# Next turn's input stage moved behind layer 1's gated unit, and two PSUM banks per VectorE instruction

## The reference, cut to what matters

```
xn = layernorm(x)
x  = x + FAVOR(xn) + LOCAL(xn)
xn = layernorm(x)
x  = x + ATTENTION(xn) + MOE(xn)
```

## Time and profile before

| what | us |
|---|---|
| median of 3 runs | 2262.85 |
| lowest and highest of them | 2262.48 to 2275.0 |
| the profiled execution, its time | 2274.8 |
| the profiled execution, its span | 2273.0 |

### The profile page before, as it was taken

How to read it: one execution, slowest core, us unless ns; L and a number is a source line. 1 busy time by engine, 2 the same in 40 slices (tenths; PEclk the granted TensorE clock), 3 DMA queues, 4 the chain that set the end, 5 groups by cost and what they waited for, 6 DMA issues and landing times.

```text
span 2273.0 us, 43389 instructions
## 1 busy us (share of the span) xinstructions
PE 1854.6 (82%) x18044; PEld 1077.6 (47%) x18044; DVE 1381.7 (61%) x2973; ACT 766.9 (34%) x1401; POOL 293.7 (13%) x238
## 2 busy tenths in 40 slices
PE   1788898788887798877988779888797887988887
PEld 1445444454454553545535444455444554444544
DVE  1666557665566664766656655666556665576654
ACT  0332253223522236233252233422343323533234
POOL 0110101101111021011110111101101101011010
PEclk9998899998999999998999989998899988999889
DMA  4000200002000020000100020000200002000020
GB/s 171 1 1 2 33 2 6 1 2 33 7 2 1 2 33 7 2 1 14 22 6 2 2 29 7 6 1 3 33 2 6 1 2 33 3 6 1 2 28 7
DMA packets 27478, 29.79 MB, mean 13 GB/s; under 512 B 3524, under 2 KB 25844, under 8 KB 26740
## 3 DMA queue, kind: packets, MB, share of 16 engines
q1 hardware_dynamic: 27284, 27.01, 6.3%
HBM read 12.06 MB, written 2.36 MB: 6 GB/s over the span
## 4 chain that ended last, share of the span: by engine, by line
PE 51%; DVE 28%; ACT 6%; SPq 5%; DMA 5%; issue 5%; POOL 0%; ACTq 0%; DVEq 0%
PE bank L913 5%; SPq L414 4%; PE bank L697 4%; PE bank L903 3%; PE bank L729 3%; DMA phi<-parts 3%; PE bank L888 3%; DVE lc L1295 2%; DVE lrec L1365 2%; DVE lc L1347 2%; DVE ftm L1276 2%; PE bank L926 2%; PE bank L998 2%; PE bank L589 2%; DVE fp L1286 2%
## 5 line engine op out<-in xcount | busy, mean ns | idle before, releaser
L1522 DVE TENSOR_REDUCE amx<-bank 128x2 f32<-128x512 f32 x256 | 163.1, 686 | 76.1 <-PE bank L926 75.9
L1143 ACT ACTIVATE silu<-bank 128x512 f32<-128x512 f32 x144 | 84.2, 597 | 275.4 <-PE bank L888 263.3
L1511 DVE TENSOR_TENSOR mh<-bank,silu 128x512 f32<-128x512 f32 x144 | 98.8, 691 | 116.8 <-PE bank L903 108.5
L913 PEld LDWEIGHTS bank<-w_mw,mh 128*128 128x128 f32 x1152 | 151.0, 210 | 24.0 <-issue 24.0
L913 PE MATMUL bank<-w_mw,mh 128*128 128x128 f32 x1152 | 158.1, 297 | 0.0
L455 POOL TENSOR_TENSOR lc<-lc,ls 128x512 f32<-128x512 f32 x32 | 40.8, 1274 | 897.8 <-DVE lc L1295 895.8
L888 PE MATMUL bank<-xn2T,w_mw 128*128 128x512 f32 x288 | 145.6, 629 | 0.0
L1543 DVE RECIPROCAL ftm<-bank 128x512 f32<-128x512 f32 x16 | 53.7, 3358 | 145.2 <-PE bank L1005 145.2
L637 PE MATMUL bank<-hT,w_wqkv 128*128 128x512 f32 x256 | 119.0, 602 | 17.2 <-ACT hT L1034 11.0
L1295 DVE SCALAR_TENSOR_TENSOR lc<-bank,w_cols,w_rotary 128x512 f32<-128x512 f32 x128 | 93.4, 746 | 59.1 <-PE bank L637 59.1
L1353 DVE TENSOR_REDUCE lmx<-bank 128x4 f32<-128x512 f32 x128 | 79.6, 685 | 80.0 <-PE bank L697 80.0
(11 more groups left out here) (265 smaller groups left out, 3709.5 us busy)
## 6 DMA issues: line engine op xcount, KB each, us to landing
phi<-parts SPq DMA_DIRECT2D x96, 64.0 KB
lc<-parts SPq DMA_DIRECT2D x96, 64.0 KB
w_mw<-in_mw SPq DMA_DIRECT2D x3, 1152.0 KB
x_in<-in_x SPq DMA_DIRECT2D x8, 256.0 KB, 9.5
out<-res SPq DMA_DIRECT2D x8, 256.0 KB, 2.3
w_wqkv<-in_wqkv SPq DMA_DIRECT2D x1, 1536.0 KB
w_w<-in_w SPq DMA_DIRECT2D x1, 682.0 KB
w_rotary<-in_rotary SPq DMA_DIRECT2D x1, 512.0 KB
```

Source lines behind the costliest of these rows:

```text
L913: last = mm(bank_of("final")[:, t], mh[:, (2 * q + i) % 4, t], W["mw2"][:, ORDER[q], i, :], start=(q == 0 and j == 0 and i == 0), stop=Fal ...
L1511: V.tensor_tensor(mh[:, n % 4, :], bank_of("moe_u", n)[:], silu[:, n % 2, :], ALU.mult).then_inc(sem["moe_h"], 1)
L1522: V.tensor_reduce(amx[:, 2 * b:2 * b + 2, h], bank_of("att_max", n)[:].rearrange("p (t k) -> p t k", t=2), AX.X, ALU.max).then_inc(sem["at ...
```

## The change

It does two things.

**The input stage of the next turn** is cut into pieces that stand earlier. SP loads the next `x_in` at the start of a turn. VectorE takes its moments in layer 0's gated unit (`input_moments`, ahead of the wait for `glu_var_ps`); the reciprocal root is made by the same eight instructions as layer 0's (eight columns in place of four), and put aside (`input_root`). `input_scale` stands in layer 1 behind FAVOR's residual. TensorE's transposes and `favor_queries` stand behind layer 1's gated unit, ahead of the wait for the second norm; so do ScalarE's copies, while its squares (`query_squares`) come ahead of the fourth expert. `favor_values` stays where it was. To allow it, the second norm goes to `ftm`, `fqk` and its squares to `lv`, and `xw` takes `cen` in place of `xnT`.

**Two banks per instruction.** The eight banks are one tensor; `pair_of_banks` makes rings start at an even bank, so that two jobs which follow each other are neighbours. Rotation is two TENSOR_TENSOR of 128x1024 per pair in place of four of 128x512, with tables `rot` of scale times rotary that are made once ahead of turn 0 (16 instructions of 128x256). Masks are 128x768, scaling is 128x1024. The maxima of group 0 are two instructions; group 1 keeps four. The bank table changes with it.

```diff
@@ the table of jobs
+        def pair_of_banks():
+            turns_of["short"] += turns_of["short"] % 2
         def favor_jobs(*slot):
             if slot in FAVOR_AT:
+                pair_of_banks()
...
-                    job("favor_score", n, "favor_p", n + 1)
+                    job("favor_score", n, "favor_p", n // 2 + 1)
...
-                job("loc_rb", 4 * l + p, "loc_qk", 8 * l + 2 * p + 2)
+                job("loc_rb", 4 * l + p, "loc_qk", 4 * l + p + 1)
...
@@ TensorE
-                    pe.wait_ge(sem["favor_p"], now("favor_p", 4 * quad + 4))
+                    pe.wait_ge(sem["favor_p"], now("favor_p", 2 * quad + 2))
...
-                        pe.wait_ge(sem["loc_qk"], now("loc_qk", 8 * l + 4 * g + 4))
+                        pe.wait_ge(sem["loc_qk"], now("loc_qk", 4 * l + 2 * g + 2))
...
+                if it + 1 < TURNS:
+                    turn_input(it + 1)
+                    favor_queries(it + 1)
                 pe.wait_ge(*freed("xn2T"))
...
-                if it + 1 < TURNS:
-                    turn_input(it + 1)
                 att_project(it, 0)
-                if it + 1 < TURNS:
-                    favor_queries(it + 1)
                 att_den(1)
@@ ScalarE
-                        act.wait_ge(sem["loc_c"], now("loc_c", n + 1))
+                        act.wait_ge(sem["loc_c"], now("loc_c", n // 2 + 1))
...
+                if it + 1 < TURNS:
+                    turn_input(it + 1)
                 act.wait_ge(sem["xn2T_ps"], now("xn2T_ps", 1))
...
+                    if q == 3 and it + 1 < TURNS:
+                        query_squares(it + 1)
                     widen(q)
@@ VectorE
+            for l in range(DEPTH):
+                for qk in range(2):
+                    for i, (trig, half) in enumerate(((0, 0), (0, 1), (1, 0), (1, 1))):
+                        ins = V.tensor_scalar(rot[:, l, qk, i, :], W["rotary"][:, 2 * qk + trig, :],
+                                              W["cols"][:, 2 + 4 * l + 2 * qk + half:3 + 4 * l + 2 * qk + half],
+                                              None, ALU.mult)
+                    made(ins)
...
+                        for n in (4 * quad, 4 * quad + 2):
+                            dve.wait_ge(sem["favor_score_ps"], now("favor_score_ps", n + 2))
+                            V.tensor_tensor(fpt2[n % 8 // 2], two_banks("favor_score", n)[:, :, 0:384],
+                                            W["causal"][:].unsqueeze(1).broadcast_to([P, 2, 384]),
                                             ALU.mult).then_inc(sem["favor_p"], 1)
...
+                        dve.wait_ge(sem["loc_raw_ps"], now("loc_raw_ps", 2 * m + 2))
...
+                        V.tensor_tensor(halves(lc[:, c:c + 2, :]), raw, tabs(0), ALU.mult)
                         if m >= 2:
                             dve.wait_ge(sem["loc_rot"], now("loc_rot", 2 * m - 2))
...
+                        V.tensor_tensor(halves(lsb[m % 2][:]), raw, tabs(2), ALU.mult).then_inc(sem["loc_c"], 1)
...
+                        c = 4 * qk + 2 * g
+                        dve.wait_ge(sem["loc_rot"], now("loc_rot", 2 * m + 2))
+                        V.tensor_tensor(lc[:, c:c + 2, :], lc[:, c:c + 2, :],
+                                        bank_of("loc_rb", m).unsqueeze(1).broadcast_to([P, 2, T]),
+                                        ALU.mult).then_inc(sem["loc_qk"], 1)
...
+                            if g == 0:
+                                dve.wait_ge(sem["loc_max_ps"], now("loc_max_ps", 8 * l + h + 2))
+                                V.tensor_reduce(lmx[:, :, i:i + 2, 0].rearrange("p j i -> p i j"),
+                                                two_banks("loc_max", 8 * l + h).rearrange("p i (j k) -> p i j k", j=TT),
+                                                AX.X, ALU.max).then_inc(sem["loc_mx"], 2)
...
+                            if it + 1 < TURNS:
+                                input_scale(it + 1)
...
+                    elif it + 1 < TURNS:
+                        input_moments(it + 1)
                     dve.wait_ge(sem["glu_var_ps"], now("glu_var_ps", l + 1))
...
-                if it + 1 < TURNS:
-                    turn_input(it + 1)
                 for b in range(G):
                     share = ftm[:].rearrange("p t d -> p (t d)")
```

More of the change, by code:

```diff
@@ L147, in build @@
         for n, ap in w.items():
[L148 removed]
+            if n not in ("ones2", "rotary", "block8", "projT"):
                 W[n] = sb("w_" + n, list(ap.shape), ap.dtype)
@@ L386, in freed @@
                 i, before, ahead = AT[name, k]
-                by, count, turn = before if before else last_in[i]
+                by, count, turn, held = before if before else last_in[i]
+                if turn and before and it + 1 == TURNS and not ahead:
+                    by, count, turn, held = held
                 turn += it - ahead - (0 if before else 1)
```

136 lines of the change are left out of this document (77 added, 59 removed).

## The result

The changed kernel took 2325.63 us (median of 5, 2310.71 to 2330.14) where the kernel before took 2267.75 in the same session: ratio 1.0239, 95% interval 1.0209 to 1.027. On the 2262.85 of the forecast that is 2317. A second series gave 1.0227 (1.0193 to 1.0261). It is slower, as forecast; the forecast's 2302 was 15 us short on that scale. The profiled execution shown here was the fastest of its series (2310.71, span 2308.9, against 2274.8 and 2273.0), while the profiled execution of before was the slower end of its own, so the rows show 36 us of the 49 to 58 that the medians lost.

A forecast was written before the change was run, and what follows sets the result against it. The bound was one long hand-over between TensorE and VectorE. Terms of 46.4 us over 8 turns, -8.4 over 7 and +1 gave 39 over 2262.85, so 2302 us; range 2252 to 2326, the forecast's own 2285 to 2320.

The forecast's parts named there:

- Turn's end: Without transposes and query products ahead of the normaliser, it starts sooner: gain 2.2 us in 7 turns.
- Price of a double instruction: A 128x1024 VectorE product in a row takes 1.14 us, bounds 1.0 and 1.3; a 128x512 one takes 0.608.
- Rotation: Waiting for the second raw half and second square delays TensorE's sums: +1.2 us per turn in layer 0, +1.6 in layer 1.
- First maxima: Masks wait for scaling to free their banks, making scores or maxima later: +1.8 us per turn in layer 0, +1.2 in layer 1.
- Gated unit, layer 0: Moments of 1.55 us stand where VectorE was just in time; +0.8 in 7 turns, bounds +0.2 and +1.5.
- Scale: In layer 1 the input scale, ahead of a reciprocal the projection waits for, has no cover: +1.1 us in 7 turns.
- Clock behind the gated unit: Work added in TensorE's wait behind layer 1's gated unit partly keeps the clock up: gain 0.9 us in 7 turns, bounds 0 and 3.1.
- rival 1: The clock stays up behind the gated unit, giving 3.1 us per turn and not 0.9: 2287 us; chance 0.14.
- At nothing: No cost from ScalarE's squares ahead of expert 3, SP's earlier `x_in` load, its absence behind the stack's transfers, or VectorE's norm.
- Rival 4: The clock also falls ahead of layer 0's first scores, +1.9 us in 8 turns: 2317 us; chance 0.18.
- Rival 2: Faster: only VectorE's busy time counts, as double products reach ScalarE and TensorE in existing holes: 2211 us; chance 0.13.
- rival 3: Both signs cancel: the maxima's bank waits cost half, the squares 0.25 us; 2265 us, chance 0.15.

The follow-up runs named there:

- experiment 10: Kernel before with double rotation alone, plus one overwritten 128x512 product per turn in layer 1 ahead of the first sums; ratio 1.0139 to the kernel before.
- experiment 2: The change without its input stage: double rotation, masks, scaling and group 0's maxima with the new banks; 2347.85 us, ratio 1.0329 to the kernel before.
- experiment 3: Kernel before with double instructions in rotation alone, banks as before; 2310.17 us, ratio 1.0157.
- experiment 8: Changed kernel whole, with other banks for the scaling rows and one quad of FAVOR scores; 2328.26 us, ratio 1.0251 to the kernel before.
- experiment 11: Kernel before with other banks for layer 1's four scaling rows, an edit of the bank table alone; 2257.61 us, ratio 0.9941.
- experiment 1: Kernel before with the new input stage alone, single-bank instructions and banks as before; 2281.23 us against 2274.06, ratio 1.0032.
- experiment 7: Experiment 1 with the moments between layer 0's two output additions and the scale between layer 1's; 2265.55 us, ratio 0.9984 to the kernel before.
- experiment 5: Experiment 1 with two more overwritten 128x512 products per turn, in TensorE's waits in and behind layer 1's gated unit; 2270.78 us, ratio 0.9997 to the kernel before.
- experiment 12: Kernel before with the input stage's moments and scale in VectorE's waits and layer 1's scaling rows in other banks, no double instructions; 2246.49 us, ratio 0.989.
- experiment 4: Kernel before with double masks, scaling and group 0 maxima alone, rotation as before, banks dealt in pairs; 2310.35 us, ratio 1.0154.

## Why the prediction was right, and where not

The sign, and the time within the range, came out. Against its own steps:

*Turn's end, -2.2:* -2.17 in the turns concerned, in every kernel with the stage moved. Right.

*Price of a double instruction, 1.14 in a row:* four in a row took 4.60 (1.15 each), two took 2.35, a single one 1.217. Right; from PSUM it costs the same as from SBUF.

*Rotation, +1.2 and +1.6:* +1.09 and +1.57 in turns without a fall of the clock. Right, and experiment 10 shows the second by itself. What the step left out is that the clock can fall at the longer wait in layer 1 (experiments 2 and 3: 1.6 more in all turns). In the changed kernel it fell there only in the last turn (21.03 from the end of layer 0's gated unit to layer 1's root, where the other turns have 19.52), which lacks the input stage's moments. So the two parts of the change do interact, and through the clock.

*First maxima, +1.8 and +1.2:* +1.97 in the lowest turn, +2.04 in the mean, and +1.21. Right in size, in layer 1 with some luck: there the scores start 1.08 later behind the scaling and the last maximum comes 0.47 later behind the first, while the clock makes the scores shorter (4.1 to 4.6 in before, 3.1 to 3.4 in after) and part of what follows longer. Experiments 8 and 11 show the wait where the forecast had it.

*Gated unit, layer 0, +0.8:* mis-sized. It was 1.3 in the mean. The forecast gave the root's wait a cushion of 1.1 (L802 at 1513.28 "wanted" it then) and counted 0.4 there. The moments put `ra` 1.36 later in all seven turns. TensorE came to L823 1.92 behind `ra` in each of them; in before it came to L802 2.76 behind it in the turn shown, but 1.88 to 3.17 over the eight turns. So the cushion was 0.84 in the turn that the forecast read, and nothing in the turn of before in which the clock was at 1.00 throughout. Two turns of experiment 1 with the clock at 1.00 throughout, the third with the moments and the last without, take 38.12 and 36.29 from FAVOR's reciprocal to the unit's end: at the upper level the moments cost 1.8.

*Scale, +1.1:* +1.02 in the turns concerned; 0.00 once it was hidden (experiment 7). Right.

*Clock behind the gated unit, -0.9 of a possible -3.1:* this failed as a size. In the first profile all seven turns kept the upper level: -3.1, rival 1's mechanism, and one of the three signs (L877's passes at 1.9 in most turns) by which the prediction said it would be wrong. It is not a property of the added work, though: the same work kept it in some turns of experiment 1 only. Half of L877's loss, taken between the bounds, had no mechanism behind it and was wrong for this kernel; over the seven turns of experiment 1 the stretch gave 1.5 in the mean.

*At nothing:* ahead of turn 0 the +1 was not there: the table products lie wholly in the wait, and the first `w_w` product starts at 48.18 (48.14 in the earlier trace rows):

```profile
48.18 1.06 DVE L1230 TENSOR_SCALAR w_w<-w_w,w_cols 128x682 f32<-128x682 f32 x2
```

But the attention's maxima came 0.8 to 1.2 later per turn in each of the six kernels with the input stage moved (experiments 1, 5, 7, 8, 12 and the change), and in none of the others; they wait for the stack's transfers. The forecast put ScalarE's squares and the missing `x_in` behind those transfers at nothing. Which of the two it is, or a third thing, stays open: SyncE issues the last `phi<-parts` 16.2 to 16.9 behind the first part in before, after and experiment 7 alike, but the maxima start 11.3 after its issue in after and 10.5 in experiment 7, where it was 9.7 in before (means of turns 1 to 7, which in before lie between 8.0 and 10.9), and the last turn, which has neither squares nor `x_in`, shows it in some kernels and not in others. No experiment separated them.

*Rival 4, chance 0.18:* it happened beside the forecast. Layer 0's first scores ran partly at the lower level (3.60 in the turn shown and up to 4.11 for 2.63), and FAVOR's reciprocal behind them came 1.28 later (rival 4's price: 1.9). It belongs to the masks, scaling and maxima (+1.13 in experiment 4), and goes when the scores start beside the scaling (experiment 8: +0.10).

The sum of the forecast is therefore near the measured one by errors of opposite sign: per turn, the clock behind the gated unit gave 2.2 more than counted, and the attention 1.9, for which there is no mechanism, while layer 0's scores and FAVOR's reciprocal took 1.3, the attention's maxima 1.1 and the gated unit 0.5. That these cancel is luck. The 13 to 22 us by which medians exceed the profiled 36 were not caught in a profile: the second shows 6 of them, in part where the clock fell in a turn. The 22 is made of two parts: the profiled execution of before was 7 over the median of its series (at a granted clock of 0.929), that of after 15 under (at 0.937, where the other four have 0.924 to 0.932). So the difference goes with the granted clock; that the time is lost by the clock alone is argued from this, and shown in no turn. Rival 2 (VectorE's rate decides) is excluded by experiments 3 and 4, rival 3 (signs cancel) by the result and experiment 2. Two of the prediction's sums come out otherwise when they are done again: rival 3 gives 2263 and not 2265, and the forecast's own range, from its bounds taken as independent, 2279 to 2316 and not 2285 to 2320.

## What to carry to other kernels

A double-width instruction saved 0.07 us of VectorE each (0.19 in the rotation, where the operation changed too). It made others wait in two places: it starts only when the second half of its input is there, and whoever needs its first half waits for both. Merge instructions only where neither neighbour is on the path. Look at the bank table before the instructions: four banks renumbered gained 14 us where the double instructions cost 74, and an input stage that cost 7 us cost nothing (-4) once its pieces stood in waits of the engine that runs them. And here an edit in one stretch moved the falls of the granted clock in others: read every turn of the same stretch, not one, and compare lowest turns before believing a mean.

## What was not expected of the hardware

The granted clock behind the same instructions and the same idle time was at 2.4 GHz in one turn and at 1.2 in the next of one execution (experiment 1: L886 1.96 and 3.76). It fell behind 1.13 us of idle in one place (experiment 5) and stayed up behind 2.08 in another (after, six or seven turns of seven). So in this kernel the idle time just ahead of a stretch doesn't tell whether the clock falls, and several stretches have two or more discrete lengths: 24.3 and 26.0 up to layer 0's root in before, 25.4 and 27.1 in after. One instruction across two PSUM banks cost what it costs from SBUF (1217 and 1219 ns for 1024 columns).
